# A decoder layer with experts: early expert tiles taken from the first four groups, a 224-column up product, exponentials turned tile by tile

## The reference

```python
x = x + linear_attention(layernorm(x))          # 8 heads, feature map elu + 1
x = x + cross_attention(layernorm(x), ctx)      # 77 context tokens; one head, tiled 16 times
x = x + experts(layernorm(x))                   # 8 experts, top 2
# cross attention: scores normalised over the 77 keys before the softmax
sigma = std(scores, ddof=1);  scores = (scores - mean) / (sigma + 1e-8)
# experts: a capacity of cap = 4096 * 2 * 1.25 / 8 = 1280 rows each
pos = cumsum(onehot(top_i)) - 1;  keep = pos < cap
h = rows @ W1;  h = gelu(h[:, :1024]) * h[:, 1024:];  out = h @ W2
```

## Time and profile before

| | us |
|---|---|
| median of 3 runs | 1474.22 (1474.14 to 1477.27) |
| the profiled execution's own time | 1474.55 |
| its span | 1472.8 |
| PE busy | 1430.7 (97%) |
| DVE, ACT, POOL busy | 640.8, 591.7, 374.8 |
| mean granted clock of PE | 0.993 |

### The profile page before, as it was taken

The page is one execution under the profiler, slowest core; times in us unless marked ns, Lnnn a source line. Parts: engine busy times, 40 slices in busy tenths (PEclk is TensorE's granted clock), DMA queues, the critical chain, the costliest instruction groups (busy, mean ns, idle before and its releaser), DMA issues.

```text
span 1472.8 us, 22222 instructions
## 1 busy us (share of the span) xinstructions
PE 1430.7 (97%) x7508; PEld 1210.8 (82%) x7509; DVE 640.8 (44%) x1379; ACT 591.7 (40%) x1018; POOL 374.8 (25%) x365
## 2 busy tenths in 40 slices
PE   7999999989989999999999999999999999999997
PEld 5768887778876888889889888899889888898886
DVE  7535666657777563123524421166223420253111
ACT  5534554258776552223424421255323321252212
POOL 3302232137666412203202211121301111021111
PEclk9999999999998999999999999999999999999999
DMA  6331223218658764204505421156504412052112
GB/s 206 60 64 30 86 87 58 86 33 209 172 133 221 176 186 108 42 2 85 151 34 123 107 64 34 21 157 189 132 7 118 103 57 43 7 152 54 21 36 28
DMA packets 82854, 135.64 MB, mean 92 GB/s; under 512 B 33234, under 2 KB 33362, under 8 KB 81780
## 3 DMA queue, kind: packets, MB, share of 16 engines
q1 hardware_dynamic: 65428, 97.68, 23.2%
q0 software_dynamic: 17376, 37.30, 13.8%
HBM read 94.41 MB, written 40.55 MB: 92 GB/s over the span
## 4 chain that ended last, share of the span: by engine, by line
PE 90%; DVE 3%; ACT 2%; issue 2%; DMA 1%; POOL 1%; SPq 0%; POOLq 0%; DVEq 0%; ACTq 0%
PE pg L1050 16%; PE pg L1052 16%; PE pg L1051 16%; PE pj L1050 10%; PE pj L1051 10%; PE pj L1052 10%; PE pj L1289 2%; PE pg L1317 2%; PE pt L1458 2%; PE pg L1255 2%; PE pt L1276 1%; PE pt L1071 1%; DMA out_rows<-ost,etab 1%; DVE kf L1582 1%; PE pt L1201 1%
## 5 line engine op out<-in xcount | busy, mean ns | idle before, releaser
L1050 PE MATMUL pg<-xe_hi,w_hi 128*128 128x512 f32 (+2 forms) x1152 | 401.7, 349 | 3.0 <-DVE xe_lo L1534 1.9
L1051 PE MATMUL pg<-xe_lo,w_hi 128*128 128x512 f32 (+2 forms) x1152 | 401.1, 348 | 0.0
L1052 PE MATMUL pg<-xe_hi,w_lo 128*128 128x512 f32 (+2 forms) x1152 | 401.0, 348 | 0.0
L1994 DVE TENSOR_TENSOR hp<-gl,pg 128x512 f32<-128x512 f32 x136 | 93.5, 688 | 569.9 <-ACT gl L1021 569.9
L728 POOL DMA_INDIRECT out_rows<-ost,etab x62 | 99.6, 1606 | 721.7 <-ACT ost L1005 359.0
L1021 ACT ACTIVATE gl<-pg 128x512 f32<-128x512 f32 x136 | 81.3, 598 | 410.9 <-PE pg L1052 410.9
L1050 PEld LDWEIGHTS pg<-xe_hi,w_hi 128*128 128x128 f32 x1152 | 218.5, 190 | 29.0 <-issue 2.8
L1051 PEld LDWEIGHTS pg<-xe_lo,w_hi 128*128 128x128 f32 x1152 | 218.5, 190 | 25.0
L1052 PEld LDWEIGHTS pg<-xe_hi,w_lo 128*128 128x128 f32 x1152 | 218.5, 190 | 25.0
L1050 PE MATMUL pj<-w_hi,hg_hi 128*128 128x512 f32 x448 | 177.0, 395 | 0.0
L1052 PE MATMUL pj<-w_hi,hg_lo 128*128 128x512 f32 x448 | 174.5, 389 | 0.0
(11 more groups left out here) (250 smaller groups left out, 1992.8 us busy)
## 6 DMA issues: line engine op xcount, KB each, us to landing
stage<-w SPq DMA_DIRECT2D x96, 512.0 KB, 4.1
xr<-x SPq DMA_DIRECT2D x8, 1024.0 KB, 10.6
out_rows<-xr SPq DMA_DIRECT2D x8, 1024.0 KB, 7.3
x_rows<-xn SPq DMA_DIRECT2D x8, 1024.0 KB, 7.1
x_in<-x SPq DMA_DIRECT2D x7, 1024.0 KB, 6.0
x_rows<-zrow POOLq DMA_DIRECT2D x1, 2304.0 KB, 15.7
late_xT<-xT_hi SPq DMA_DIRECT2D x2, 1024.0 KB, 3.9
late_xT<-xT_lo SPq DMA_DIRECT2D x2, 1024.0 KB, 6.0
```

Source lines behind the costliest of these rows:

```text
L1050: nc.tensor.matmul(o, lh, rh, start=start, stop=False)
L1051: nc.tensor.matmul(o, lh, rl, start=False, stop=False)
L1052: return nc.tensor.matmul(o, ll, rh, start=False, stop=stop)
L1994: v.tensor_tensor(hp[j % 2][:], gl[j % 2][:], pg[:, 2 + j % 2, :], ALU.mult).then_inc(s_hp, 1)
```

## The change

`SOON` goes from 6 to 4: the early tiles come from groups 0 to 3, are fetched at the end of group 4, and are turned and split in group 5 (`SOON_TURNED`) into tiles of their own, `soon_xe_hi` and `soon_xe_lo`; a bank of `pt` that held them is waited for by `s_xelo`. The up widths are listed in `UP_WIDTHS`, 224, 384 and 512, and chosen by nested comparisons. `score_exp` signals each of its four tiles, and `turn_exp` waits for each. `sigma` takes the variance to the power 1/2 in one POOL operation; the factor sqrt(77/76) goes into the DVE instruction that adds epsilon.

```diff
...
 CHUNKS = [4, 4, 2]
+UP_WIDTHS = [2 * P - 32, 3 * P, 4 * P]
...
 BANK = {s: 0 if place == 2 else 1 for (g, place), jobs in LATE_AT.items() for s in jobs}
...
-SOON, SOON_TILES = GROUPS - 2, 2
+SOON, SOON_TILES = GROUPS - 4, 2
+SOON_TURNED = SOON + 1
...
     soon_hi = alias("soon_hi", [P, FJ, SOON_SLOTS], F32R, one_at + 8192 * 5 + 4096)
+    soon_xe_hi = alias("soon_xe_hi", [P, KC, SOON_SLOTS], F32R, one_at + 8192 * 7)
+    soon_xe_lo = alias("soon_xe_lo", [P, KC, SOON_SLOTS], F32R, one_at + 8192 * 7 + 4096)
...
           sp.dma_start(out_g[g], xr[g % 4][:]).then_inc(s_out, 16)
-          if g == SOON:
+          if g == GROUPS - 2:
...
       def sigma(g):
...
           pool.wait_ge(s_s2, g + 1)
-          step(p.tensor_scalar(sig[:, 0], mv2[:, :, 1], CK / (CK - 1.0), None, ALU.mult))
-          p.tensor_tensor(sig[:, 1], sig[:, 0], half_pos[:], ALU.pow).then_inc(s_sig, 1)
+          p.tensor_tensor(sig[:, 1], mv2[:, :, 1], half_pos[:], ALU.pow).then_inc(s_sig, 1)
...
                            scale=rstd[1][:, i:i + 1]).then_inc(s_xn3, 1)
...
-      def rows_hi(first, tiles):
+      def rows_hi(first, tiles, to):
...
               act.wait_ge(s_xet, first + i + 1)
-              a.activation(xe_hi[:, :, i * P:(i + 1) * P],
+              a.activation(to[:, :, i * P:(i + 1) * P],
...
       def score_exp(g):
...
           for i in range(TI):
-              ins = a.activation(sc[:, i, :], sc[:, i, :], ACT.Exp, bias=nbias[:, i:i + 1],
-                                 scale=sig[:, 3, i:i + 1])
-          ins.then_inc(s_e, 1)
+              a.activation(sc[:, i, :], sc[:, i, :], ACT.Exp, bias=nbias[:, i:i + 1],
+                           scale=sig[:, 3, i:i + 1]).then_inc(s_e, 1)
...
               turned_rows(xT2, range(2, TI), 1)
+          if g == SOON_TURNED:
+              rows_hi(0, range(SOON_TILES), soon_xe_hi)
           if g == GROUPS - 1:
-              rows_hi(0, range(SOON_TILES))
...
           if i == 0:
-              rows_hi(SOON_TILES, range(CHUNKS[0]))
+              rows_hi(SOON_TILES, range(CHUNKS[0]), xe_hi)
...
               ins.then_inc(s_o, 1)
...
-      nt, last = [0], [0, 0]
+      nt, last, soon_turned = [0], [0, 0], [0, 0]
...
       def bank(k):
...
               pe.wait_ge(s_btev, last[k])
+          if soon_turned[k]:
+              pe.wait_ge(s_xelo, soon_turned[k])
...
       def turn_exp(g):
-          pe.wait_ge(s_e, g + 1)
...
           for i in range(TI):
+              pe.wait_ge(s_e, g * TI + i + 1)
...
               ins.then_inc(s_xet, 1)
+              soon_turned[i] = i + 1
...
           values(g, range(2, TI))
-          if not more_groups:
+          if g == SOON_TURNED:
               turn_soon()
-              positions(g)
+          positions(g)
           if more_groups:
-              positions(g)
...
                   ins = three(pg[:, 2 * half + j % 2, 0:SOON_SLOTS], w1_hi[:, j, k, m], w1_lo[:, j, k, m],
-                              xe_hi[:, k, 0:SOON_SLOTS], xe_lo[:, k, 0:SOON_SLOTS], k == 0, k == KC - 1)
+                              soon_xe_hi[:, k, :], soon_xe_lo[:, k, :], k == 0, k == KC - 1)
...
               following = pe.snap(first + 2 + (c < 2) * 2, min_val=2, max_val=EX * ET + 14)
...
-              def up(tiles):
-
-                  w = tiles * P
+              def up(w):
...
                          stop=True).then_inc(s_y, 1)
...
-              with pe.If(left < 2 * P + 1):
-                  up(2)
-              with pe.Else():
-                  with pe.If(left > 3 * P):
-                      up(4)
+              def up_narrowest(widths):
+
+                  if len(widths) == 1:
+                      up(widths[0])
+                      return
+                  half = len(widths) // 2
+                  with pe.If(left < widths[half - 1] + 1):
+                      up_narrowest(widths[:half])
                   with pe.Else():
-                      up(3)
+                      up_narrowest(widths[half:])
+
+              up_narrowest(UP_WIDTHS)
...
       def softmax(g):
...
           dve.wait_ge(s_sig, g + 1)
-          link(v.tensor_scalar(sig[:, 2], sig[:, 1], SIG_EPS, None, ALU.add))
+          link(v.tensor_scalar(sig[:, 2], sig[:, 1], (CK / (CK - 1.0)) ** 0.5, SIG_EPS, ALU.mult, ALU.add))
...
           v.tensor_tensor(gate[:, :, 1, 1], ge[:], gate[:, :, 0, 1], ALU.mult).then_inc(s_dest, 1)
...
-      def rows_lo_of(first, tiles):
+      def rows_lo_of(first, tiles, lo, hi):
...
               dve.wait_ge(s_xehi, first + i + 1)
-              low(xe_lo[:, :, i * P:(i + 1) * P], pt[i % 2][:].rearrange("p (k t) -> p k t", k=KC),
-                  xe_hi[:, :, i * P:(i + 1) * P]).then_inc(s_xelo, 1)
+              low(lo[:, :, i * P:(i + 1) * P], pt[i % 2][:].rearrange("p (k t) -> p k t", k=KC),
+                  hi[:, :, i * P:(i + 1) * P]).then_inc(s_xelo, 1)
...
               positions_out(g)
+              if g == SOON_TURNED:
+                  rows_lo_of(0, range(SOON_TILES), soon_xe_lo, soon_xe_hi)
...
               cross_out(g)
-              rows_lo_of(0, range(SOON_TILES))
...
               counts()
-      rows_lo_of(SOON_TILES, range(CHUNKS[0]))
+      rows_lo_of(SOON_TILES, range(CHUNKS[0]), xe_lo, xe_hi)
...
...
```

## The result

The changed kernel takes 1487.22 us (median of 4 runs, 1484.75 to 1488.61) against 1474.18 beside it (1473.51 to 1477.27): a ratio of 1.0082, 95% interval 1.0063 to 1.0102. It is slower, as forecast, but by 13.0 us and not by 7.0, and 1.2 us above the range. Its profiled execution took 1487.24 us with a span of 1485.5, 12.7 longer than before's.

A forecast was written before the change was run, and what follows sets the result against it. TensorE (PE), busy 97% of the span and throughout the expert loop, was taken as the bound. Terms +12.9 - 1.9 + 1.6 - 0.95 - 0.65 - 4.0 = +7.0 us gave 1481.2 us, range 1477.5 to 1486.

The forecast's parts named there:

- the line: Expert loop: up products cost a straight 0.0805 us a column per set, 0.42 ns a column per matmul, also below 256.
- the floor: Rival, narrow up sets: load and product never under 114 ns, so 7.7 us gain becomes 3.3; time 1485.6; chance 0.10.
- Two sets from 256 to 384: Expert loop: third chunks of experts 1 and 3, exactly 256 rows each, go to 384 columns; +20.6 us.
- Three sets to 224: Expert loop: chunks of 155, 207 and 148 rows (experts 0, 2, 6) go from 256 to 224 columns; -7.7 us.
- Groups 0 to 2: Group loop: sigma in one POOL operation and exponentials turned tile by tile shorten PE's idle time; -1.9 us.
- Group 5: PE waits some 0.75 us for ACT's x1 copies, then turns the early tiles; positions and scores come later; +1.6 us.
- group 6: Shorter sigma and tile-by-tile turning of the exponentials, with the clock at 0.50, cut PE's idle time; -0.95 us.
- Group 7: Shorter sigma and tile-by-tile turning of the exponentials, nothing lying between; -0.65 us.
- the tail: Group 7 without the early tiles' work: gate difference 5.3 us earlier, third early product 4.6 earlier; -4.0 us beyond group 7's 0.65.
- Width hardly matters: Rival, expert loop: matmuls cost nearly the same at 256 and 384 columns; time 1472.3, no change; chance 0.02.
- The clock holds: Rival, groups 6 and 7: less idle time keeps PE's clock up, giving back 1.2 and 2.0 us; time 1478.0; chance 0.12.
- The rival with the narrow width for the third chunks: Every third chunk, including experts 1 and 3, takes the narrow width; price 25.8 us, time 1455.4, chance 0.03.

The follow-up runs named there:

- e9: Kernel before the change, its narrowest up body streaming 128 columns instead of 256 in five chunks, leaving rows out; 1469.58 us, ratio 0.9979.
- e11: Kernel before the change, its narrowest up body streaming 224 columns instead of 256 in five chunks, 32 rows of two left out; 1467.76 us, ratio 0.9950.
- e2: Changed kernel with the up widths of before (256, 384, 512), all its other edits kept; 1472.41 us, ratio 0.9986.
- e7: Kernel before the change with only the early tiles taken from groups 0 to 3, fetched after group 4, turned in group 5; 1478.11 us, ratio 1.0011.
- e3: Kernel before the change with only the up widths 224, 384 and 512; 1492.40 us, ratio 1.0115.
- e6: Kernel before the change with only sigma in one POOL operation and the exponentials turned tile by tile; 1476.11 us, ratio 0.9992.
- e10: Kernel of e2 plus idle PE products, 2 ahead of the turning in group 6 and 5 in group 7; 1471.39 us, ratio 0.9990.
- e8: Kernel of e2 plus idle PE products: 9 ahead of group 6's turning, 3 behind group 7's, 8 ahead of the third early product; 1487.21 us, ratio 1.0063.
- e4: Changed kernel with narrow sets of 128, 160 and 208 columns plus 256, 384, 512; 20 rows left out; 1689.74 us, ratio 1.1468.

## Why the prediction was wrong

Its direction and its reason were right. Two things failed in the sum: the price of the narrow sets (-7.7 forecast, -4.8 measured), and a loss that it put at nothing, 1.9 us behind expert 0's set. The first alone, 1481.2 + 2.9 = 1484.1, would have stayed in the range. For the first the text had the number: 114 ns for a pair of load and product at 96 columns. It then said "That row has other operands (plain fp32), so I take the line", and gave the floor a chance of 0.10. The floor it was. The row was also read a little high: 3.66 us over 32 takes in the last product's full length. Its starts, in the timeline of before, show the floor itself:

```profile
321.67 3.51 PE L1289 MATMUL pj<-wqk,xT 128*128 128x96 f32 x30
...
325.02 0.28 PE L1289 MATMUL pj<-wqk,xT 128*128 128x96 f32 x1
```

Thirty steps in 3.35 us are 111.7 ns each: with other operands, the rate that the narrow up sets then showed.

- *Two sets from 256 to 384, +20.6*: 10.3 each, +20.6. Right.
- *Three sets to 224, -7.7*: 1.6 each, -4.8. Wrong by 2.9, and shown by e9 and e11: 111.4 to 112.1 ns a pair at 128 and 224 columns, 120 at 256. The line of 0.42 ns a column ends between 224 and 256. The Trainium skill (TensorE: Matmul & The Clock Gate, section LDWEIGHTS) gives a weight load P / 1.2 ns for its P columns, 107 at 128. If a pair could not be faster than its load, which the section does not say, that would be such a floor, by estimate; the traces put it 5% higher. At 107 ns 224 columns would still have cost what the line says, so that figure alone would not have mended the sum. That the load is what sets the floor is not shown here.
- *Expert 0's set counted like the others*: its 1.6 us came, and 1.6 us were lost at half clock behind the turning, with 0.27 more of waiting. No term had it. The loop from expert 0's up set on is +17.8 us in place of +12.9: 2.9 from the floor, 1.9 from the clock and the wait, 0.1 not placed.
- *Groups 0 to 2, -1.9*: the turning of group 3 comes 2.13 us earlier, of which 0.82 was there before the first scores, where no term had it; -1.3 is left.
- *Group 5, +1.6, and group 6, -0.95*: from the turning of group 5 to that of group 6 21.88 instead of 21.43, +0.45 against +0.65. PE waits 0.71 us for ACT's copies (0.75 predicted). Late query sums end at 433.6 and hold nothing up.
- *Group 7, -0.65, and the tail, -4.0*: from the turning of group 6 to the third early product 35.56 instead of 39.26, -3.7 against -4.65. All before the loop is then -5.4, -5.9 predicted. The next in line was named ("If a weight piece were"), and in e2 and e7 it was the weight piece. So that after comes this near is also luck. In its profile the clock held in group 7's values (3.68 us, 5.54 before), in e2 and e10 it fell there as before; e2, the same but for the widths, starts expert 0's up set 1.6 us earlier and not 5.4, and its interval (5.2 below to 0.9 above) leaves out the 5.9 forecast.
- *The rivals*: the floor is what happened (1485.6 forecast for it), together with a clock loss that none had. *Width hardly matters* was wrong (a third of the loop's 12.9 is 4.3, not 4.0; it would still have been no change). *The clock holds* came half true and cost elsewhere. The rival with the narrow width for the third chunks did not happen.

The profiled spans differ by 12.7, 5.7 more than forecast: 2.9 from the floor, 1.9 from the clock and the wait, 0.5 from what lies before the loop, and 0.4 in the loop and behind it that are not placed. The range failed because its upper end stood at the floor alone (1485.6) and left no room for a second loss on top of it.

What stays open: why the clock falls behind the first turning. It fell in after, e2, e7, e9 and e11 behind idle times of 1.76 to 2.40 us, and held in before, e3, e6 and e10 behind 1.76 to 2.13. Neither the wait's length, nor the set's width, nor the early tiles separates the two groups. Each is one execution; whether it changes from one to the next of the same kernel is not shown.

## What to carry to other kernels

Before a width is narrowed, look for the narrowest pair of load and product that the trace holds, and take its rate as a floor until a row shows a faster one. A list of widths that replaces one of them prices every chunk that sat exactly on the old value. And a further variant in a run-time choice can cost even when it is never taken: watch the instruction queue's packets in the loop.

## What the runs showed of the hardware that was not expected

- The instructions of a loop count as a whole: 1464 on PE ran 17 chunks with 5 packets fetched in 900 us, 1865 with 40 and with stalls of 0.5 to 3.8 us ahead of most up sets, 2667 with stalls of up to 16.5 us. The count is not the whole rule: e8, with 1464, fetched 9 and stalled twice.
- A set of load and product pairs can run at half clock for nearly all its length while PE never idles: the 160-wide one of e4, 20.00 of 20.00 us busy at 0.50, behind a wait of 2.62 us. Only its first 2 us or so, of 39, were at 1.00. The 128-wide one of the same run had 1.00.
- Half-clock stretches behind waits of 2 to 4 us lasted 3 us in some executions and ten in others, in the same group. So a difference of some 3 us in front of the loop, between two single profiles, need not come from an edit.
